# The sixth batch's normalisation moved into the expert blocks, and one of the last loads made an adding one

## The reference

```python
out = 0.5 * gelu(flat @ shared_W + shared_b)
for e in range(n_exp):
    h = gelu(flat @ W1[e] + b1[e])
    out = out + combine[:, e:e + 1] * (h @ W2[e] + b2[e])
mean = out.mean(axis=-1, keepdims=True)
var = ((out - mean) ** 2).mean(axis=-1, keepdims=True)
out = (out - mean) * rsqrt(var + LN_EPS) * gamma + beta     # the inner normalisation
...
x = x + _layernorm(out)                                      # the outer one
```

## Time and profile before

| | us |
|---|---|
| median of 3 runs | 757.47 |
| the runs | 765.1, 757.47, 756.79 |
| the profiled execution | 752.52 |
| its span | 750.8 |

### The profile page before, as it was taken

One profiled execution on the slowest core, in us unless ns is written; L12 is line 12 of the kernel. 1 busy time (PEld: TensorE's weight loads), 2 busy tenths in 40 slices (PEclk: granted clock), 3 DMA queues, 4 the chain that ended last, 5 costly groups with the idle time before them and its releaser, 6 DMA issues.

```text
span 750.8 us, 17408 instructions
## 1 busy us (share of the span) xinstructions
PE 647.7 (86%) x5255; PEld 547.4 (73%) x5255; DVE 458.5 (61%) x1243; ACT 460.2 (61%) x879; POOL 299.9 (40%) x389
## 2 busy tenths in 40 slices
PE   4779789889887799987988999999999998999930
PEld 3567567667765587866867889998998997887820
DVE  4479878797887563523345544444444445777777
ACT  2657647557555483743555666766675555788975
POOL 4000332432526612464572434544453564534421
PEclk9989999898998899988898999999999999999985
DMA  7563553550155332111112122222111396433567
GB/s 254 170 252 111 172 167 101 182 170 31 61 166 198 85 114 71 44 45 57 37 52 81 59 69 79 84 74 72 58 51 44 78 200 141 78 66 60 115 166 140
DMA packets 46600, 79.88 MB, mean 106 GB/s; under 512 B 17905, under 2 KB 31538, under 8 KB 46130
## 3 DMA queue, kind: packets, MB, share of 16 engines
q1 hardware_dynamic: 33954, 47.17, 19.7%
q0 software_dynamic: 12560, 31.60, 17.9%
...
## 4 chain that ended last, share of the span: by engine, by line
PE 65%; DVE 12%; issue 9%; ACT 8%; DMA 2%; another core or an unknown queue 2%; POOL 1%; ACTq 1%; DVEq 1%; POOLq 0%
PE banks L479 15%; PE banks L480 14%; PE banks L481 14%; PE banks L916 4%; PE banks L850 4%; ACT X L1390 3%; PE banks L869 2%; PE banks L873 2%; DMA X<-y_rows 2%; PE banks L990 2%; PE banks L950 1%; PE banks L899 1%; DVE st L1916 1%; PE banks L934 1%
## 5 line engine op out<-in xcount | busy, mean ns | idle before, releaser
L1390 ACT ACTIVATE X<-banks,b1T,tab 128x256 f32<-128x256 f32 x312 | 157.3, 553 | 144.9 <-PE banks L481 110.2
L1859 DVE SCALAR_TENSOR_TENSOR stage<-X,tab,stage 128x512 f16<-128x512 f32 x156 | 115.7, 751 | 121.0 <-ACT stage L1395 75.9
L479 PE MATMUL banks<-X,W 128*128 128x256 f16 x624 | 172.0, 276 | 10.7 <-DVE X L1866 6.4
L479 PE MATMUL banks<-W,stage 128*128 x624 | 173.0, 277 | 7.2 <-issue 5.7
L753 POOL DMA_INDIRECT y_rows<-X,tb x78 | 87.6, 1123 | 224.0 <-DVE X L1882 209.8
L480 PE MATMUL banks<-W,stage 128*128 x624 | 173.0, 277 | 3.2 <-issue 3.2
L481 PE MATMUL banks<-W,stage 128*128 x624 | 173.1, 277 | 2.8 <-issue 2.7
L480 PE MATMUL banks<-X,W 128*128 128x256 f16 x624 | 171.8, 275 | 0.0
L481 PE MATMUL banks<-X,W 128*128 128x256 f16 x624 | 171.7, 275 | 0.0
L1395 ACT ACTIVATE stage<-X,tab 128x512 f16<-128x512 f32 x156 | 112.6, 722 | 11.3 <-ACT X L1390 7.0
L742 POOL DMA_INDIRECT X<-xf_rows,tb x78 | 89.7, 1149 | 32.4 <-issue 24.8
...
## 6 DMA issues: line engine op xcount, KB each, us to landing
...
```

What stands on the lines that cost most here:

```text
L479: pe.matmul(o, lh, rh, start=first, stop=False)
L1390: a.activation(h32[:, m % 2, r * BT:(r + 1) * BT], PS[m][:, r * BT:(r + 1) * BT], ACT.Gelu, bias=b1T[:, bass.ds(e * NH + 2 * m + r, 1)], s ...
L1859: v.scalar_tensor_tensor(o[1], src, tab[:, 1, bass.ds(e, 1)], o[0], ALU.mult, ALU.subtract).then_inc(h_low, 1)
```

## The change

1. **Batch 5 moves into the blocks.** `inner_stats(5)` goes from block 37 to block 34, its root and factors get a group of their own (blocks 35 and 36), `inner_norm(5)` is in block 37 and `gamma_beta(5)` and `outer_stats(5)` in block 38, ahead of `last_result(0)`. `outer_norm(2)` goes from block 37 to behind block 38, `add_out(2)` from block 36 to block 37 of POOL's list, which puts it between scatter 37 and scatter 38.
2. **Batch 7's first results come by an adding load.** POOL issues it into `ub[7]` as soon as all scatters have landed; SP loads only the second; DVE adds only one. The semaphore `out_added` counts the new transfer with the first three `add_out`.
3. **Statistics rearranged.** `inner_stats` of batches 0 to 4 move behind the result of their block or a block on, `inner_factors(0)` from block 31 to 32, `outer_factors(0)` from 35 to 36, and `add_rows(0, 1)` from block 27 to 26. In the tail `outer_norm(5)` goes ahead of `roots(1, 2)`.

```diff
-INNER_GROUPS = ((0, 20), (20, 28), (28, 30), (30, 32))
-OUTER_GROUPS = ((0, 12), (12, 20), (20, 28), (28, 30), (30, 32))
+INNER_GROUPS = ((0, 20), (20, 24), (24, 28), (28, 30), (30, 32))
+OUTER_GROUPS = ((0, 12), (12, 24), (24, 28), (28, 30), (30, 32))
...
+            sp.dma_start(last_y[1].rearrange("p t d -> p (t d)"), yv[1, B - 1]).then_inc(final_in, 16)
             for k in range(2):
-                sp.dma_start(last_y[k].rearrange("p t d -> p (t d)"), yv[k, B - 1]).then_inc(final_in, 16)
...
                 if j == 26:
                     for b in range(3):
                         add_rows(b, 0)
+                    add_rows(0, 1)
                 if j == 27:
-                    for b in range(3):
+                    for b in range(1, 3):
                         add_rows(b, 1)
...
                 if j == 36:
                     add_out(1)
+                if j == 37:
                     add_out(2)
-            g.wait_ge(final_in, 16 * 3)
+            g.wait_ge(u_gelu, B)
+            g.wait_ge(y_stored[0], 16 * HALVES * ((NB + 1) // 2))
+            g.wait_ge(y_stored[1], 16 * HALVES * (NB // 2))
+            g.dma_start(ub[B - 1].rearrange("p t d -> p (t d)"), yv[0, B - 1], accum_op=ALU.add).then_inc(out_added, 16)
+            g.wait_ge(out_added, 16 * 4)
+            g.wait_ge(final_in, 16 * 2)
...
                 if j == 35:
                     a.preload_act_table(ACT.Sqrt)
                     roots(1, 0)
+                    roots(0, 1)
                     a.preload_act_table(ACT.Gelu)
                 if j == 36:
                     outer_norm(0)
                 if j == 37:
+                    inner_norm(5)
                     outer_norm(1)
+                if j == 38:
                     outer_norm(2)
             a.preload_act_table(ACT.Sqrt)
+            roots(0, 2)
             roots(1, 1)
-            roots(0, 1)
-            inner_norm(5)
             inner_norm(6)
             outer_norm(3)
             outer_norm(4)
+            outer_norm(5)
             roots(1, 2)
-            outer_norm(5)
             outer_norm(6)
...
-                for k in range(2):
-                    v.tensor_tensor(o, o, last_y[k][:, lo:hi, :], ALU.add).then_inc(final_sum, 1)
-                    v.wait_ge(final_sum, lo + k + 1)
+                v.tensor_tensor(o, o, last_y[1][:, lo:hi, :], ALU.add).then_inc(final_sum, 1)
+                v.wait_ge(final_sum, lo // 2 + 1)
...
-                if 29 <= j < 32:
-                    inner_stats(2 * (j - 29))
+                if 30 <= j < 32:
+                    inner_stats(2 * (j - 30) + 1)
+                if j == 32:
+                    inner_factors(0)
+                if j == 34:
+                    inner_stats(5)
+                if j == 36:
+                    outer_factors(0)
+                    inner_factors(1)
+                if j == 38:
+                    gamma_beta(5)
                 result(j - 1)
...
-                if 29 <= j < 31:
-                    inner_stats(2 * (j - 29) + 1)
-                if j == 31:
-                    inner_factors(0)
+                if 29 <= j < 32:
+                    inner_stats(2 * (j - 29))
                 if 32 <= j < 37:
                     gamma_beta(j - 32)
                     outer_stats(j - 32)
-                if j == 35:
-                    outer_factors(0)
-                if j == 37:
-                    inner_stats(5)
                 if j == 38:
+                    outer_stats(5)
                     last_result(0)
                     inner_stats(6)
             last_result(1)
-            inner_factors(1)
+            inner_factors(2)
             outer_factors(1)
-            gamma_beta(5)
             gamma_beta(6)
-            outer_stats(5)
             outer_stats(6)
             outer_factors(2)
-            v.wait_ge(final_in, 16 * 3)
-            v.wait_ge(u_gelu, B)
+            v.wait_ge(final_in, 16 * 2)
+            v.wait_ge(out_added, 16 * 4)
             add_last(0, 2)
```

9 lines of the change are left out of this document (4 added, 5 removed).

## The result

| | before | changed |
|---|---|---|
| median of 4 runs, us | 761.29 | 768.64 |
| the runs, us | 765.1, 757.47, 756.79, 765.99 | 770.9, 772.02, 764.83, 766.38 |
| profiled execution, us | 752.52 | 770.9 |
| its span, us | 750.8 | 769.2 |
| mean granted clock of TensorE | 0.938 | 0.929 |

The changed kernel is slower: the ratio is 1.0145, with a 95% interval of 1.0097 to 1.0192. The forecast was 760.8 us with a range up to 764.5, so the measured 768.64 lies outside it.

A forecast was written before the change was run, and what follows sets the result against it. TensorE was taken to pace the blocks and DVE's order to set the end. Terms of -0.5, +4.4, +1.5, +1.3, -2.2, -1.4 and +0.2 gave +3.3 on 757.47, so 760.8 us, range 756.0 to 764.5.

The forecast's parts named there:

- blocks 27 to 38: Expert blocks: early gain mostly spent by added DVE and ACT work; GELU 38 at 709.3 for 709.79, -0.5 us.
- last result, from block 38: Behind block 38: DVE's new order ends the last result's second half at 726.1 for 722.20, +4.4 us.
- from the value to the landed scatters: POOL's end: `add_out(2)` queues ahead of the last scatters, which land at 731.5; 5.4 against 3.9, +1.5 us.
- the load, less its slack: Batch 7's adding load: 7.0 us against 5.7 for two plain loads, +1.3, less 2.2 of slack used up.
- two adds less: DVE's stage behind the last load: two adds drop out at 0.7 to 0.75 each, -1.4 us.
- stores beside the adds to `out`: Kernel end: the four `add_out` finish at 751.2, just ahead of the end beside the last stores, +0.2 us.
- gain at block 33: 3.5: Block 33: GELU starts near 651.5 instead of 655.3, a gain of 3.7 taken as 3.5 us.
- the bill of block 31, undisturbed: Blocks 31 and 32: GELU 31 at 621.9, its last split 7.7 later, GELU 32 near 636.4 for 641.26.
- Hidden transfers (A): End: scatters don't queue behind `add_out(2)`, adding load costs like a plain one; +0.6, 758.1 us, chance 0.2.
- A surviving early gain (B): DVE in blocks 34 and 36 absorbs its added 2.8 us, so the change is faster; -1.3, 756.2 us, chance 0.09.
- POOL blocked in block 26 (C): `add_rows(0, 1)` waits, delaying scatter 27 and gather 31, for which TensorE waits; +6.5, 764.0 us, chance 0.12.
- Nothing of note (D): Whole kernel: gains and losses meet within 0.5 us; 757.5 us, chance 0.09.

The follow-up runs named there:

- repeated: The changed kernel run once more, unedited, beside the kernel before: median +5.19 us against it, ratio 1.0101 [1.0062, 1.0139].
- the kernel with all repairs: Changed kernel with batch 5's late DVE work behind the last result, `add_out(2)` and unheld adds behind the adding load, `inner_norm(6)` ahead of outer roots: 1.0019 of before.
- The experiment on `add_out(2)`: Changed kernel with `add_out(2)` sent behind the last scatter instead of ahead of it: median +8.72 us against before, ratio 1.0043 [0.9992, 1.0094].
- the combined kernel: Kernel before plus the rearranged statistics and the adding load, adds to `out` not held by it: median -1.97 us against before, ratio 0.9968 [0.9938, 0.9998].
- the statistics alone: Kernel before with only batches 0 to 4's statistics rearranged and batch 0's adds earlier: two executions, -4.41 and -1.59 us, ratios 1.0036 and 0.9973.
- batch 5 behind: Changed kernel with `gamma_beta(5)` and `outer_stats(5)` put behind both halves of the last result on DVE: median +4.99 us against before, ratio 1.0049 [1.0018, 1.0080].
- adds unheld: Changed kernel with a separate semaphore for the adding load, so POOL's four adds to `out` don't wait for it: +6.39 us against before, ratio 1.0093.
- plain loads: Changed kernel with both of batch 7's results loaded plainly again and DVE adding both: median +5.32 us against before, ratio 1.0073 [1.0046, 1.0100].

## Why the prediction was wrong, step by step

| step of the sum | forecast | first profile | repeated |
|---|---|---|---|
| blocks 27 to 38 | -0.5 | +1.06 | +0.22 |
| last result, from block 38 | +4.4 | +3.93 | +3.93 |
| from the value to the landed scatters | +1.5 | +1.02 | +0.82 |
| the load, less its slack | -0.9 | -0.83 | +0.41 |
| two adds less | -1.4 | -1.44 | -1.45 |
| stores beside the adds to `out` | +0.2 | +2.90 | +1.73 |
| sum | +3.3 | +6.6 | +5.7 |

The columns are differences of landmarks against the first profile of before; the load is taken from the landed scatters (SP's plain load) to DVE's first add. As an example, the last row is 769.2 - 763.78 = 5.42 less 750.8 - 748.28 = 2.52. For the repeated execution it is 760.3 - 756.05 = 4.25 less 2.52.

**Wrong, the largest part: "just ahead of the end but beside the last stores: +0.2".** The adds to `out` were forecast to be through 12.7 us behind the first; they started at 751.11 and kept the engines full to 763.5 to 764, which is 12.4 to 12.9. The forecast also put that within 3 us of the end. Two things it did not ask. The first is who else uses the engines in these 3 us: the stores of the last batch, 262 GB/s when they are alone. Before, 2 us of idle DMA lay between the two; the change used them up, and the stores land 2.0 us late (0.8 in the repeated execution). The second is when POOL itself is through. The row that was read, still shows the adds at a DMA share of 0.84 and not their end; POOL's last row ended 748.6 - 731.8 = 16.8 us behind the first add, not 12.7, and from 738.5 that is 755.3, past the forecast's own end of 754.1. In the changed kernel it ended 17.8 and 16.8 behind it and closed the span, 0.9 us later than the stores would have. The price of both is 1.7 to 2.9 us. Taking the hold away brought the gap between last add and end back to 2.5, and the kernel with all repairs ends 2.4 us behind its last add (33.78 - 31.34).

**Wrong, the smaller part: "gain at block 33: 3.5".** The order of payments was right. `inner_stats(5)` was put at 1.67 and cost 1.66 to 1.68. The root in block 35 was put at 0.3 and cost 0.2 (12.10 against 11.93 from 35 to 36). The factors in block 36 were put at 1.1 and cost 1.0 (12.43 against 11.43 from 36 to 37). But what they were paid from was smaller. At block 32 the forecast had 641.26 - 636.4 = 4.9 and the gain was 3.0 and 3.8; at block 33 it had 3.5 (3.8 by its own figures, 655.3 - 651.5) and the gain was 1.7 and 2.6. The step that failed is "the bill of block 31, undisturbed": it let blocks 30 and 31 pass at 10.93 each. From 29 to 31 they took 45.27 - 22.05 = 23.22 and 45.04 - 21.86 = 23.18, 1.3 more than 21.86. It also had the last split of block 31 end 7.7 us behind that block's first GELU; it ended 9.3 behind it (642.15 + 1.41 - 634.24), and ACT waited 0.90 us for DVE in the same block (638.74). DVE does two batches' statistics and a result between the splits of block 30 and those of block 31 (632.40 to 637.2), so I read the loss as statistics that are not hidden; no run took these two apart. In the first profile block 28 took 0.9 more (11.85 against 10.93) and block 29 gave 0.7 of it back (22.05 against 21.85 for both).

**Right: DVE's order.** The last half was forecast 16.8 us behind block 38's first GELU. It ended 738.95 - 722.62 = 16.3 behind it. Put back alone, it gave the 4.0 back and the end came 3.0 to 3.1 earlier.

**Right: POOL's queue in order.** The scatters were put at 731.5 on a first GELU at 709.3, 22.2 behind; SP's load stands at 743.86 - 722.62 = 21.2. The experiment on `add_out(2)` showed the order itself.

**Right in kind, low in size: the adding load.** It was put at 7.0, counted from the landed scatters. It took 7.0 and 8.3 in the changed kernel, 7.5 to 8.6 in the edited ones where DVE waited for it, and at most 8.1 when done alone (730.84 to 738.90), against 4.8 to 5.7 for two plain ones. In the combined kernel, where DVE did not wait, it landed 6.7 behind the scatters (742.7). That it came out at 7.0 in the first profile is partly luck: of the six times that DVE waited it is the lowest, and the repeated execution has 1.3 more. The other estimate, 3.2 us by the Trainium skill, "DMA: Bandwidth & Descriptors", section "Anatomy of one DMA", is not borne out by any run here.

**The rivals.** Hidden transfers (A): no, DVE waited 2.79 and 3.84 us for the load. A surviving early gain (B): no; even the statistics alone keep only 1.1 to 3.0, and the change spends them. POOL blocked in block 26 (C): it did wait 3.11 us at 613.58, as C had it, but no wait of TensorE for a gather followed, and block 30 to 31 went faster than before. So the wait was there and cost nothing. C's time of 764.0 is nearer to the measurement than the forecast is, but by another mechanism. Nothing of note (D): no, the medians differ by 5.2 and 7.4. The chance of "slower" had been 0.06; by the line of 7.6 us drawn there the medians stay just inside, and the ratio of the first pair, 1.0145, is outside.

**The footing.** The sum was put on 757.47, the median of three executions. The fourth moved it to 761.29. A range that leaned on three executions lying 8 us apart should have been wider for that alone, and on the side of the two higher ones. With the range at 764.5, all four executions of the changed kernel lie above it, and two of the kernel before.

**Left open.** Both profiles of before close block 27 at 585, the changed kernel at 597 and 589, all the edited kernels between 589 and 599. Most of that cannot be the change's: the differences of medians for the change itself (+5.2 and +7.4) are within 1 us of the landmarks' sums. But four kernels edited from the changed one (batch 5 behind, `add_out(2)` behind, adds unheld, plain loads) have medians 1.6 to 3.0 us above theirs, and the repaired one 0.8, where those edited from the kernel before lie between 1.4 below and 1.4 above. So 1 to 2 us ahead of block 27 may be the change's, or medians of 10 to 12 executions are no better than that; no run took it apart. The granted clock of the first 270 us was 0.91 and 0.89 in the first two profiles, which goes with it; what sets it was not tried.
